# Four token steps per routing decision instead of two, in a graph network, Mamba and mixture-of-experts kernel

## The reference, cut to what matters

```
x = x + L0_gnn(layernorm(x), adj)      # convolution, gaussian attention, GRU
x = x + L0_ffn(layernorm(x))           # Mamba-2 block
# L1_gnn: graph convolution
d = (sum(adj, -1) + 1e-5) ** -0.5
x = x + (d * adj * d^T) @ (layernorm(x) @ weight) + bias
# L1_ffn: mixture of 8 experts, each token goes to its best two
flat   = layernorm(x).reshape(-1, 128)
probs  = softmax(flat @ router_w.T)
p2, i2 = top_k(probs, 2);  p2 = p2 / (sum(p2) + 1e-9)
gates  = sum_k p2[k] * onehot(i2[k])
y_e    = (silu(flat @ w1[e].T) * (flat @ w3[e].T)) @ w2[e].T
x = x + sum_e gates[e] * y_e
```

## Time and profile before

| what | value |
|---|---|
| median of 3 runs | 1268.82 us (1266.85 to 1269.21) |
| the profiled execution | 1267.55 us, its span 1265.5 us |
| PE, DVE, ACT, POOL busy over the span | 83%, 68%, 56%, 33% |
| mean granted TensorE clock | 0.887 of full speed |
| first and last instruction of `dispatch_phase` | 767.43 and 931.76 us (POOL) |
| first scatter | 831.44 us |
| first load of `expert_phase` | 940.49 us |

### The profile page before, as it was taken

One profiled execution on the slowest core, in us unless ns is written; L12 is line 12 of the kernel. 1 busy time (PEld: TensorE's weight loads), 2 busy tenths in 40 slices (PEclk: granted clock), 3 DMA queues, 4 the chain that ended last, 5 costly groups with the idle time before them and its releaser, 6 DMA issues. The chain is left out here.

```text
span 1265.5 us, 23407 instructions
## 1 busy us (share of the span) xinstructions
PE 1044.5 (83%) x6778; PEld 915.9 (72%) x6778; DVE 862.1 (68%) x2186; ACT 714.8 (56%) x1566; POOL 412.2 (33%) x415
## 2 busy tenths in 40 slices
PE   1999999999995856888997785577319999799997
PEld 1988889898884823566665574466319999699996
DVE  4576767677658538999999955799825555355553
ACT  3566565656552247888888835666215555355553
POOL 4233232323216500001000012556733444434444
PEclk9999999999995577888889877788559999899999
DMA  4121213121001022222222106553334444233331
GB/s 155 52 75 43 83 41 83 41 75 50 33 1 28 0 71 67 56 57 55 68 67 67 35 1 200 144 159 102 111 97 127 146 126 130 78 91 97 97 98 42
DMA packets 83146, 99.54 MB, mean 79 GB/s; under 512 B 9595, under 2 KB 68994, under 8 KB 82922
## 3 DMA queue, kind: packets, MB, share of 16 engines
q1 hardware_dynamic: 72778, 74.70, 21.7%
q0 software_dynamic: 8832, 21.26, 4.8%
q10 hardware_dynamic: 1440, 2.40, 0.5%
HBM read 72.70 MB, written 27.21 MB: 79 GB/s over the span
## 5 line engine op out<-in xcount | busy, mean ns | idle before, releaser
L1596 PE MATMUL e_p_y<-w,e_gT 128*128 (+1 forms) x864 | 119.8, 275 | 0.0
L862 POOL TENSOR_TENSOR m_rs<-m_ms,m_minus_half 128x4 f32<-128x4 f32 x16 | 23.2, 1450 | 295.3 <-ACT m_ms L895 295.3
L1543 DVE TENSOR_TENSOR e_g<-e_sl,e_p_h 128x342 f32<-128x342 f32 x144 | 73.6, 511 | 64.7 <-ACT e_sl L1521 58.7
L1596 PEld LDWEIGHTS e_p_y<-w,e_gT 128*128 128x128 f32 (+1 forms) x864 | 107.6, 191 | 0.4 <-issue 0.4
L87 PE MATMUL e_p_h<-w_hi,e_xT_hi 128*128 x288 | 106.0, 368 | 1.4 <-DVE e_g L1543 0.8
L1525 ACT ACTIVATE e_gT<-e_p_gx 128x384 f32<-128x384 f32 x144 | 70.7, 491 | 64.5 <-PE e_p_gx L1586 64.5
L1521 ACT ACTIVATE e_sl<-e_p_h 128x342 f32<-128x342 f32 x144 | 65.9, 457 | 70.8 <-PE e_p_h L89 70.8
L1547 DVE TENSOR_TENSOR e_xT_lo<-e_p_gx,e_xT_hi 128x128 fp32r<-128x128 f32 x144 | 42.0, 292 | 90.3 <-ACT e_xT_hi L1529 89.8
L1507 POOL DMA_INDIRECT sorted_scratch<-e_xg x72 | 70.0, 972 | 97.5 <-DVE e_xg L1553 95.9
L1505 POOL DMA_INDIRECT out<-e_xg x72 | 69.8, 970 | 90.7 <-DVE e_xg L1553 84.6
L955 DVE SCALAR_TENSOR_TENSOR m_c<-m_p_x,m_vecs,m_c 128x506 f32<-128x506 f32 (+2 forms) x144 | 95.6, 740 | 0.0
(11 more groups left out here) (357 smaller groups left out, 3380.2 us busy)
## 6 DMA issues: line engine op xcount, KB each, us to landing
e_xg<-sorted_scratch SPq DMA_DIRECT2D x144, 130.0 KB, 2.1
m_cum<-cum_scratch SPq DMA_DIRECT2D x16, 1024.0 KB
g_adjT<-in_adjT SPq DMA_DIRECT2D x16, 512.0 KB, 3.9
g_adj<-in_adj SPq DMA_DIRECT2D x16, 512.0 KB, 4.9
c_adjT<-in_adjT SPq DMA_DIRECT2D x16, 512.0 KB, 6.3
x_tokens<-in_x SPq DMA_DIRECT2D x16, 256.0 KB, 4.9
sorted_scratch<-nothing SPq DMA_DIRECT2D x2, 1040.0 KB, 9.8
sorted_scratch<-nothing SPq DMA_DIRECT2D x12, 130.0 KB, 2.4
```

The source lines that it names most:

```text
L1543: dve.tensor_tensor(g[:, i % D3], sl[:, i % 2], p_h3[i % 2][:, 0:HP], ALU.mult).then_inc(q["g_ready"], 1)
L1596: last = pe.matmul(p_y[d % 2][:, 0:P], gT[0:r, d % D3, k], w2k[:, bass.ts(e, P)], start=k == 0, stop=k == len(CH) - 1)
```

## The change

GROUP goes from 2 to 4. The picks, the destination part, the rank products and the exponentials then run four times on four steps (TG = 16 tiles) instead of eight times on two (TG = 8 tiles), at iterations 10, 14, 18, 22 and 11, 15, 19, 23. The tiles `logits`, `gap`, `hot`, `upto` and `p_rank` become twice as wide, and each group issues 16 scatters in a row instead of 8. The table `restart`, which makes the scan start again for each expert, gets 16 ones behind each zero. Lags, loops and waits are written as before; their counts follow from GROUP.

```diff
     NORM2 = OUT + 1
     TURN2, COPY2, LOG, TAKE = OUT + 2, OUT + 3, OUT + 3, OUT + 4
-    GROUP = 2
+    GROUP = 4
     TG = GROUP * T
     PICK, DEST = TAKE, TAKE + 1
...
-        "restart": np.tile(np.array([0.0] + [1.0] * 8, np.float32), TOPK * EX),
+        "restart": np.tile(np.array([0.0] + [1.0] * 16, np.float32), TOPK * EX),
```

## The result

The changed kernel takes 1290.11 us (median of 4 runs, 1288.88 to 1291.74), the kernel before 1268.19 us beside it (4 runs): ratio 1.0173, 95% interval 1.0157 to 1.0189, so 21.9 us slower. The forecast was 1291. The profiled execution took 1291.15 us, with a span of 1289.3 us.

What follows compares the result with a forecast made beforehand. POOL's chain of scatters was taken to set the phase's end. Start 843.1 plus bursts 20.5, 20.5 and 41.4 and gaps 16.1 and 12.6 gave 954.2 against 931.76, +22.4 us, hence 1291 us; range 1283 to 1299.

Steps and rivals of the forecast that it cites:

- Part 1: DVE's picks and destination parts: 44.2 us become 27.5, up to 17 us, a gain only if DVE sets the end.
- Part 2: POOL's first scatter, in iteration 11 instead of 9: at 843.1, 11.7 us later; bounds 840.2 and 846.65.
- the ring: The loop between ACT and DVE, which sets the pace of iterations without picks: 5.15 us a step.
- Part 3: POOL's gap after the first 16 scatters, DVE standing at L1321 for the queued bias addition: 16.1 us, bounds 12 and 19.
- The disputed term: Whether three bias additions in a row hold DVE's L1325 in the first gap: no gives 16.1 us, yes 18.6.
- Part 4: POOL's gap after the second burst, with step 15 as the last: 12.6 us, bounds 11 and 15.
- Part 5: Phase end: groups 3 and 4 give 32 scatters in a row, 41.4 us as now; barrier and expert phase stay.
- The sum: End of POOL's last scatter: start, bursts and gaps add to 954.2 against 931.76, +22.4 us; start +11.7, gaps +10.8.
- (a): Rival: DVE is the bound from 831 to 891, so the kernel gets 16.7 us faster, 1252; chance 4%.
- (b): Rival: only the first scatter's late start counts, gaps keep their 17.9 us; loss 11.7 us, 1280.5; chance 8%.
- (c): Rival: lighter DVE work makes up for the later start, no change, 1269; chance 2%.
- (d): Rival: stalls feed each other, a late product delays one gap by 5.15 us, 1296, or both, 1301; chance 12%.

Runs made afterwards that it cites:

- spread scatters: Each group's scatters issued four per iteration, bias addition between: in the changed kernel (four steps) 1276.73 us, ratio 0.9998; in the kernel before (two steps) 1275.37, ratio 0.9982.
- the control: The kernel before, unchanged, run again on the chip where it takes 1277 us: 1278.26 us, ratio 1.0014.
- the mixed groups: Changed kernel with groups of 4, 4, 2, 2, 2, 2 steps, step s scattered in iteration s + 11: 1270.60 us against 1268.07, ratio 1.0030.
- the four-step kernel without bias: Changed kernel without POOL's bias addition (L1201) and DVE's wait for it: 1288.82 us, ratio 1.0080; repeated on the other chip 1264.77, ratio 0.9977.
- one step to a group: GROUP = 1 instead of the kernel before's 2, plus one DVE wait for ACT's exponential: 1300.44 us against 1277.16, ratio 1.0185.
- the late scatters: Kernel before, groups of two, with POOL's scatters two iterations later: 1290.68 us, ratio 1.0090; repeated on the other chip 1274.33, ratio 1.0055.

## Why the prediction was right

**Part 1, DVE's work.** Right, and the costs of wider tiles too. DVE's forms in the changed kernel over 765 to 960 us, against the earlier trace rows:

```profile
L1351 DVE TENSOR_TENSOR_SCAN c_upto<-c_restart,c_hot 128x272 f32<-128x272 f32 x4 | 2.9, 724 | 0.1
L1348 DVE TENSOR_TENSOR c_pick<-c_pick,c_rev 128x128 f32<-128x128 f32 x4 | 1.2, 292 | 0.1
```

Predicted were 461 + 128 x 2.1 = 730 ns and 233 + 64 x 1.03 = 299 ns. A pick takes 4.63 us (869.89 to 874.52) for 4.52. DVE's busy time over the phase fell from 134.0 to 115.2 us, 18.8 for 16.7. L1360, which I had left out because the bias additions hold it, alone fell from 7.8 us in all to 1.7 (8 x 972 ns, 4 x 430 ns); what took some of that back I did not follow.

**Part 2, the first scatter.** 845.91 instead of 843.1, inside the bounds. Of the 2.8 us, 1.75 arose far ahead: iteration 8's update starts at 819.16, not 817.41. They are lost in iterations 3 and 4, at the output products of the first two steps, where PE ran at its lower clock for longer: the granted clock from 777 to 783 us was 1.00 in the kernel before and 0.58 in the changed one. PE's timeline of the changed kernel:

```profile
777.15 2.05 PE L1407 MATMUL c_p_out<-c_weight,c_aggT 128*128 128x128 f32 x8 [0.78 <-ACT c_aggT L1262]
778.99 3.41 PE L1415 MATMUL c_p_agg<-c_adjT,c_xs 128*128 128x256 f32 x8
```

and of the kernel before:

```profile
776.99 1.13 PE L1407 MATMUL c_p_out<-c_weight,c_aggT 128*128 128x128 f32 x8 [1.04 <-ACT c_aggT L1262]
777.96 1.89 PE L1415 MATMUL c_p_agg<-c_adjT,c_xs 128*128 128x256 f32 x8
```

The same eight matmuls in 2.05 and 1.13 us, near the ratio of 2.4 and 1.2 GHz. PE's instructions up to there are the same in both kernels, and in both it had stood idle for 8.64 us ahead of the product at 772.6. The changed kernel's second trace and both kernels with spread scatters, that with two steps too, show 2.05 us; the control, the mixed groups and the four-step kernel without bias show 1.13. So it isn't bound to the group's size; what decides it stays open. The other 1.0 us is nearly all in the ring: its two steps took 5.20 and 6.03 us, for 5.15 each; the second waited 1.80 us for ACT's rough root.

**Part 3, the first gap.** 16.14 us for 16.1, and by its own steps: addition to update 1.31 us (1.28), update and statistics 2.23 (2.2), pick 4.63 (4.5), head of iteration 15 1.91 (2.0), second update 2.23 (2.2), then L1360 until the addition of step 14 ends, 13.3 us behind the burst (13.25), 2.0 us of destinations and 0.80 to hand over. DVE stopped for 10.42 us (about 10). The disputed term came out on the side I took. Three additions run from 866.35 to 870.06, and L1325, beside the second of them, takes 1.13 us, as without them; L1360, with both inputs in SBUF, takes 0.69 us beside one addition where it takes 0.17 us alone. The rule of the Trainium skill (SBUF — State Buffer, "Who interferes with whom") for one SBUF input and for two agrees with both rows. By the other reading, my sum for the gap would have been 18.6.

**Part 4, the second gap.** 12.69 us for 12.6. The two rank products ran from 911.04 to 913.14, 2.10 us for 2.35, and DVE waited 0.21 us for them, not 0.5. The five small instructions of iteration 19's head (0.88 us), which I had dropped with the statistics, took the difference. Two errors that cancel.

**Part 5, the end.** 32 scatters without a stop, in 40.6 us for 41.4: in the kernel before three of them (914.68 to 918.99) had taken 1.0 to 1.4 us busy instead of 0.97. **The sum:** start +14.5 for +11.7, gaps 28.8 for 28.7, scatters 81.2 for 82.5; 955.9 for 954.2. In the kernel before I had counted four bursts at 10.25 us, but only the first takes that (10.23) and the others 9.9 to 10.0: it has 81.6 us of scatters and 18.7 of gaps, not 82.4 and 17.9, so the gaps grew by 10.1 us. That the median came out within 1 us of the forecast is partly luck: the phase grew by 24.2 us in the traces, for 22.4, the medians differ by 21.9, and the changed kernel's profiled execution lay 1.0 us above its median, where that of the kernel before lay below.

**The rivals.** (a), DVE the bound: the DVE time was saved and the kernel is 21.9 us slower; only with one step to a group is DVE the bound. (b), only the start counts: the gaps are 28.8 us, not 17.9; the start alone gives 6.3 us, and with the order mended some 7 of 24 us of the phase's growth are left (estimate above). (c), hidden: no. (d), a larger loss: its first link, a product late at the lower clock, did appear, ahead of the place I gave it, and cost 1.75 us, not 5.15.

What the prediction had right for a weaker reason is the split of the sum. "Start +11.7, gaps +10.8" adds up, but the two aren't independent: delaying the scatters by 12.8 us cost 6.3, since later gaps close. The experiments split the loss otherwise: some 6 to 7 us for the late start, 15 to 18 for the burst ahead of the bias addition. Had I used my split to judge a repair, I would have said that the late start alone loses 11.7 us, and that spreading the scatters saves at most 10.8; it saves 17 to 18.

## What to carry to other kernels

When a loop written out by hand makes one engine issue a batch, look for what stands behind the batch on that engine and who waits for it: a batch is harmless up to the slack of that consumer (here two iterations, 10 us, for eight scatters of 10.2 us), and beyond it the consumer stands still (here for 10.4 and 11.7 us behind sixteen scatters of 20.4). Making a batch larger to spare its producer can be paired with issuing it in slices, which here took back 17 to 18 us of the loss but not the late start. For the end of a chain count the backlog as well as the waits: the end is when the last wait is over, plus all that is then left to issue. And take the control for an expectation from traces that nothing else disturbs: here one such comparison gave 8 us where 4 were there.

## What the runs showed of the hardware

- A scatter of 128 rows costs POOL 1.28 us (0.97 busy, 0.30 between) in bursts of 4, 8, 16 and 32 alike, but for the first of a kernel (1.26 busy) and a few single ones of up to 1.40 us busy.
- Chips can differ by more than many a change: the kernel before takes 1268.1 us on one and 1277.2 on the other. In traces of the second, engines wait in places, for up to 13.7 us, with "remote" as the releaser, which means that the trace finds no instruction that ended the wait, and for 0.3 to 1.2 us for their own preceding instruction. Waits of ACT in the control, from 831 to 900 us; the trace of the kernel before on the other chip has none of them:

```profile
ACT c_aggT L1262 <- remote: 6.2, 1, 6.2
ACT c_xs L1253 <- remote: 5.1, 1, 5.1
```

  Their cause is open. They fall at different places in each trace and cost kernels unequally: by the medians 9 us for the kernel before, 5 for the changed one, 16 for the late scatters and 24 for four steps without bias. The two experiments with the largest shares pointed the wrong way until they were repeated; the spread scatters, one step to a group and two steps with spread scatters were run on that chip only.
- PE's step to the higher clock can come later with the same PE instructions before it: the granted clock from 777 to 783 us was 1.00 in one trace and 0.58 in another, and the work behind it came 1.75 us later (Part 2).
